# Two feed-forward products by Strassen's algorithm, with the sums of operands and products made beside them

## The chip, the cores and the metric

The kernel runs on one core of a Trainium2 chip. The time is the device time of one execution in microseconds (us), median of three runs. Everything is float32; the matrix products take each operand as a high and a low part (type fp32r) and add three products per pair.

## What is computed

Cut to what matters here: a cross-attention layer, and behind it a feed-forward layer on z, the normalized sum x + attention.

```python
x = x + xattn(layernorm(x), ctx)                      # x: (4, 512, 1024)
z = layernorm(x)
routing = sum(top_k(z @ gate_w, 2))                   # gate_w: (1024, 8)
h = relu(z @ up_w) ** 2                               # up_w: (1024, 2048)
shared = h @ down_w                                   # down_w: (2048, 1024)
routed = ((z @ fc1_w) @ expert_w * routing) @ fc2_w   # fc1_w: (1024, 512), expert_w: (512, 512), fc2_w: (512, 1024)
out = x + layernorm(shared + routed) * gamma + beta
```

## The kernel before, in words

The program has stages, one behind the other, with five engines that wait for each other by semaphores. Each stage has a function for each engine (`c_pe`, `c_dve`, and so on). `past(s, v)` is a semaphore and the count to wait for.

- **p0, a, b**: weights, layer norm, q, k and v, attention. The change leaves them as they are, but for two names that it takes from them.
- **c**, the output projection: 16 tiles of 128 rows (4 batches of 4). TensorE makes 12 k-steps x 2 halves x 3 parts = 72 matmuls a tile. The attention output comes from DRAM in four units a tile (`c_load_unit` on SyncE's queue). ScalarE makes a unit's high part (`c_units_hi`), GpSimd its low part (`c_units_lo`). A unit's place is free again when TensorE has used it in the tile before. VectorE adds x to the finished tile (`c_dve`, L1607), SyncE stores it. Batch 1 also folds `expert_w` and `fc2_w` into one matrix `w_d`. Beside the last two batches VectorE normalizes z of batches 0 and 1 (`d_norm`), ScalarE stores it and reads it back in blocks (`d_z_out` L1342, `d_blocks_in` L1350), and VectorE turns the blocks (`d_turn` L1362).
- **d**, the up products: for each batch 16 chunks of `up_w` and 4 of `fc1_w`, each with 8 k-steps x 3 parts = 24 matmuls of 128x512 (`mm_groups`, `D_GROUPS`). The weights are split once into a hi and a lo half in 16 slots and stay there for all batches; only the four fc1 chunks are loaded again. ScalarE applies relu, VectorE squares, ScalarE stores (`d_act`, `d_dve`). A gate product of 16 matmuls a batch is made behind the first group (L1701, L1702), behind a wait for the gate's weights (`d_gw`).
- **e**, the down products: 16 tiles of 128 rows, each 20 k-steps x 2 halves x 3 parts = 120 matmuls (`e_pe`, `step`). The weights stay on chip for all tiles. ScalarE scales the routed part by the routing weight, VectorE adds, takes the layer norm and adds x (`e_dve`, `tile`). The last tile has its second half cut into two pieces of 256 columns (`LAST`), and a chain made for it in `last_tile`.

`parts3` is where nearly all matmuls stand, L118 to L120:

```python
e.matmul(o, lh, rh, start=first, stop=False)
e.matmul(o, lh, rl, start=False, stop=False)
return e.matmul(o, ll, rh, start=False, stop=last)
```

## Time and profile before

| what | value |
|---|---|
| median of 3 runs | 2096.02 us (2095.66 to 2096.24) |
| span of the profiled execution, first to last instruction | 2094.0 us |
| own time of the profiled execution | not given; the span is 2.0 us under the median |
| TensorE busy | 2075.4 us (99% of the span), 9580 matmuls |
| VectorE, ScalarE, GpSimd busy | 803.9, 695.1, 754.5 us |
| DMA | 286.31 MB, mean 137 GB/s |

The profile has one line for each engine. A matmul's duration there is about 0.39 us for 512 columns, while the next one starts 0.23 us later: matmuls overlap in the array, so what one costs is read from the distance of the starts. The feed-forward stages take the last 43% of the span, from about 1200 us on. A group's line in the rows below gives its count, its busy time, the mean of one instruction, and the idle time ahead of it with what ended it.

### The profile page before, as it was taken

How to read it: one execution, taken by the hardware profiler on the slowest of the kernel's cores; microseconds unless marked ns; L12 is line 12 of the kernel's file. 1: busy time of each engine (PE TensorE's matmuls, PEld its weight loads, DVE VectorE, ACT ScalarE, POOL GpSimd, SP SyncE). 2: the span in 40 equal slices, each digit the busy share in tenths (PEclk: the TensorE clock that was granted, in tenths of full speed). 3: DMA queues.
4: the chain of work that ended last, by engine and by line, in shares of the span. 5: the costliest groups of instructions: out<-in, count | busy, mean ns of one | idle time of the engine just before them, and what ended most of it. 6: DMA issues, size and time to landing. Idle time of an engine off the chain costs nothing.

```text
span 2094.0 us, 30294 instructions
## 1 busy us (share of the span) xinstructions
PE 2075.4 (99%) x9580; PEld 1732.2 (83%) x9580; DVE 803.9 (38%) x1419; ACT 695.1 (33%) x1209; POOL 754.5 (36%) x616
## 2 busy tenths in 40 slices
PE   8999999999999999999999999999999999999998
PEld 7888888888888888878888878787878888888887
DVE  4221312178888888831121412313231232222222
ACT  5121111167777777741111223112123311111111
POOL 2533030147777777662222343010024322222221
PEclk9999999999999999999999999999999999999999
DMA  6843433635655655544347555253434622222222
GB/s 198 265 158 140 154 117 111 179 83 147 159 151 150 160 154 137 130 121 146 131 156 198 200 157 156 105 150 111 133 97 134 211 87 89 90 88 83 76 82 76
DMA packets 302751, 286.31 MB, mean 137 GB/s; under 512 B 146896, under 2 KB 214480, under 8 KB 301776
## 3 DMA queue, kind: packets, MB, share of 16 engines
q1 hardware_dynamic: 188128, 196.58, 30.2%
q10 hardware_dynamic: 114544, 88.76, 15.3%
q8 instruction: 40, 0.66, 0.1%
q14 instruction: 39, 0.32, 0.1%
HBM read 184.32 MB, written 100.68 MB: 136 GB/s over the span
## 4 chain that ended last, share of the span: by engine, by line
PE 94%; DMA 2%; DVE 1%; POOL 1%; ACT 1%; issue 0%; ACTq 0%; SPq 0%; DVEq 0%; POOLq 0%
PE psum L118 29%; PE psum L119 29%; PE psum L120 29%; PE psum L988 3%; DMA staging<-in_up_w 1%; POOL operands L1281 1%; PE psum L1035 1%; PE psum L1015 1%; PE psum L1034 1%; PE psum L1016 1%; DMA staging<-in_fc_w 1%; DMA staging<-in_ctx 0%; ACT operands L1276 0%; PE psum L1702 0%; PE psum L1701 0%
## 5 line engine op out<-in xcount | busy, mean ns | idle before, releaser
L118 PE MATMUL psum<-operands 128*128 128x512 f32 (+3 forms) x2904 | 1115.7, 384 | 11.4 <-DVE operands L353 10.0
L119 PE MATMUL psum<-operands 128*128 128x512 f32 (+3 forms) x2904 | 1113.6, 383 | 0.0
L120 PE MATMUL psum<-operands 128*128 128x512 f32 (+3 forms) x2904 | 1111.0, 383 | 0.0
L118 PEld LDWEIGHTS psum<-operands 128*128 128x128 f32 (+1 forms) x2904 | 546.5, 188 | 111.5 <-DVE operands L353 9.8
L120 PEld LDWEIGHTS psum<-operands 128*128 128x128 f32 (+1 forms) x2904 | 546.9, 188 | 105.4
L119 PEld LDWEIGHTS psum<-operands 128*128 128x128 f32 (+1 forms) x2904 | 547.5, 189 | 94.0
L1281 POOL TENSOR_TENSOR operands<-staging,operands 128x512 fp32r<-128x512 f32 x92 | 118.6, 1301 | 349.3 <-ACT operands L1276 348.3
L1162 DVE TENSOR_REDUCE small<-psum 128x1 fp32r<-128x576 f32 x256 | 192.9, 754 | 89.8 <-PE psum L988 89.7
L1940 POOL TENSOR_TENSOR operands<-operands 128x640 fp32r<-128x640 f32 x64 | 100.6, 1574 | 319.1 <-ACT operands L1935 318.9
L905 POOL TENSOR_TENSOR operands<-staging,operands 128x512 fp32r<-128x512 f32 x128 | 164.6, 1293 | 30.4 <-ACT operands L1082 21.6
L1791 DVE TENSOR_TENSOR staging<-staging 128x512 f32<-128x512 f32 x64 | 46.6, 747 | 327.6 <-ACT staging L1749 326.8
L1935 ACT ACTIVATE operands<-operands 128x640 fp32r<-128x640 f32 x64 | 47.3, 740 | 284.4 <-DMA operands<-h_scratch 284.4
L1496 POOL TENSOR_TENSOR operands<-operands 128x384 fp32r<-128x384 f32 x64 | 65.7, 1032 | 183.7 <-ACT operands L1491 183.3
L1075 ACT ACTIVATE staging<-psum 128x512 f32<-128x512 f32 (+1 forms) x192 | 110.4, 589 | 27.2 <-DVE psum L1190 23.6
L1276 ACT ACTIVATE operands<-staging 128x512 fp32r<-128x512 f32 x92 | 56.4, 631 | 178.5 <-DMA staging<-in_up_w 59.2
L988 PEld LDWEIGHTS psum<-operands 96*128 96x128 f32 x512 | 95.5, 189 | 23.0 <-DVE small L1162 1.7
L1082 ACT ACTIVATE operands<-staging 128x512 fp32r<-128x512 f32 (+1 forms) x192 | 112.8, 620 | 0.0
L988 PE MATMUL psum<-operands 96*128 96x288 f32 x512 | 110.2, 297 | 0.1
L907 POOL TENSOR_TENSOR operands<-staging,operands 64x512 fp32r<-64x512 f32 x64 | 82.5, 1289 | 62.7 <-ACT operands L1082 59.2
L637 DVE SCALAR_TENSOR_TENSOR staging<-psum,staging 128x512 fp32r<-128x512 f32 (+1 forms) x40 | 26.5, 662 | 189.1 <-ACT staging L632 189.1
L1071 ACT ACTIVATE psum<-psum 128x512 f32<-128x512 f32 x128 | 74.6, 583 | 62.9 <-PE psum L120 59.6
L1491 ACT ACTIVATE operands<-operands 128x384 fp32r<-128x384 f32 x64 | 33.1, 524 | 177.8 <-DMA operands<-o_scratch 170.5
(123 smaller groups left out, 1285.0 us busy)
## 6 DMA issues: line engine op xcount, KB each, us to landing
h_scratch<-staging ACTq DMA_DIRECT2D x80, 256.0 KB, 2.2
operands<-h_scratch SPq DMA_DIRECT2D x64, 320.0 KB, 3.1
operands<-recip_scratch SPq DMA_DIRECT2D x64, 192.0 KB, 4.0
o_scratch<-staging SPq DMA_DIRECT2D x64, 192.0 KB, 4.9
operands<-o_scratch SPq DMA_DIRECT2D x64, 192.0 KB, 2.9
operands<-q_hi_scratch ACTq DMA_DIRECT2D x14, 768.0 KB, 5.9
operands<-q_lo_scratch ACTq DMA_DIRECT2D x14, 768.0 KB, 6.0
staging<-in_x SPq DMA_DIRECT2D x20, 512.0 KB, 4.0
```

The costliest lines, as they stand in the source:

```text
L118: e.matmul(o, lh, rh, start=first, stop=False)
L119: e.matmul(o, lh, rl, start=False, stop=False)
L120: return e.matmul(o, ll, rh, start=False, stop=last)
L905: e.tensor_tensor(pt[j][1], pst[j // 2], raw(pt[j][0]), ALU.subtract).then_inc(b_lop, 1)
L907: e.tensor_tensor(pt[j][0][C:P], pst[j // 2][0:C], raw(pt[j][0][0:C]), ALU.subtract).then_inc(b_lop, 1)
L988: m = e.matmul(bank[:, h * TH:(h + 1) * TH], qp[p][0][0:HD, a * S + u * P:a * S + (u + 1) * P], kp[p][0][0:HD, h * TH:(h + 1) * TH], start ...
L1071: e.activation(bank, bank, ACT.Exp).then_inc(b_ex, 1)
L1075: e.activation(pst[j // 2][0:n], bank[0:n], ACT.Exp).then_inc(b_ex, 1)
L1082: e.activation(pt[j][0][0:n], pst[j // 2][0:n], ACT.Copy).then_inc(b_hia, 1)
L1162: e.tensor_reduce(nm[o % 2][:, u:u + 1], bank[:, 0:T], AX.X, ALU.max, negate=True).then_inc(b_mx, 1)
L1281: e.tensor_tensor(job_part(j, h, slot_lo), halves[h], raw(job_part(j, h, slot_hi)), ALU.subtract).then_inc(j_lo, 1)
L1940: e.tensor_tensor(eu[u][1], raw(eu[u][1]), raw(eu[u][0]), ALU.subtract).then_inc(e_lo, 1)
```

## The change

It computes both feed-forward products by Strassen's algorithm (in Winograd's form of the sums), one level deep: the matrices are cut in four blocks, and seven block products take the place of eight.

- **Up products (new d).** The rows are two batches against two batches, the inner dimension is cut in two, and the columns are pairs of chunks. There are 10 iterations: 5 column blocks (4 of `up_w`, 1 of `fc1_w`) for each of two pairs of batches (`q` = 0 for batches 0 and 1, `q` = 1 for batches 2 and 3). Each has seven products in the order 1, 5, 6, 2, 7, 3, 4. Each product is 2 x 4 x 3 = 24 matmuls of 128x512. Operands: z operands (128 x 2048 each) are made once for each `q`, by VectorE's sums `z_sum`, ScalarE's high part `z_hi` and low parts by VectorE (`z_lo`, products 1, 5, 6, 7, 3) or GpSimd (`z_lo_pool`, products 2, 4). Weight operands (128 x 1024 each) are made anew in every iteration: four sums (`w_sum_op`) and three low parts (`w_lo_op`) on VectorE, seven high parts on ScalarE, four low parts (`w_lo_pool`) on GpSimd. The products' sums (seven additions from PSUM or SBUF), the four squares, and, on GpSimd, five sums of h that serve as operands of the next product (`add`) come on top. All seven operands of h are stored.
- **Down products (new e).** Seven passes (2, 4, 1, 3, 6, 5, 7), each with 8 groups (pairs of row tiles) of 10 k-steps x 3 parts = 30 matmuls of 128x512. Weights are loaded, added and split anew for each pass. Results are gathered in 16 tiles in SBUF. The layer norm of a tile is made in pass 6 or 7; the last tile is normalized whole.
- **z.** z is normalized by five jobs (`z_norm`), turned on chip, and stored turned (`z_turned_out`, `z_part_out`); it is read back as operands. Batches 0 and 1 and the norm of batch 2 lie in stage c; the rest lies in iterations 0 to 3 of stage d.
- **Gate.** 16 matmuls for batches 0 and 2, 24 for batches 1 and 3 (80 in place of 64). The wait for the gate's weights (`d_gw`) now stands ahead of stage d's first product.

The core of the diff, new code only (the old bodies of stages d and e are taken out; line numbers of the rest shift by 20 to 40):

```diff
+        ORDER = [1, 5, 6, 2, 7, 3, 4]
+        Z_SUMS, Z_HI, Z_LO_V, Z_LO_G = [5, 6, 7, 4], [1, 6, 5, 7, 2, 3, 4], [1, 5, 6, 7, 3], [2, 4]
+        W_SUMS, W_HI, W_LO_V, W_LO_G = [5, 6, 7, 3], [1, 5, 6, 2, 7, 3, 4], [5, 1, 6], [7, 2, 3, 4]
...
+        def d_first_loads(e):
+            e.wait_ge(*past(z_tw, 16))
+            z_load_op(e, 0, 1)
+            e.wait_ge(*past(z_tw, 32))
+            e.wait_ge(*past(f_lo, NQ))
+            z_stage(e, 0, "b12")
+            w_stage(e, 0)
+            z_stage(e, 0, "b22")
...
         def c_sp_eng(e):
...
+                    if n == LAST_C - 2:
+                        d_first_loads(e)
...
         def c_act(e):
...
+                if n in (7, 11):
+                    z_blocks_in(e, 2 * ((n - 7) // 4))
+                if n:
+                    c_units_hi(e, n, (2, 3))
+                if n in (7, 11):
+                    z_blocks_in(e, 2 * ((n - 7) // 4) + 1)
...
+                if n in (9, 13):
+                    z_turned_out(e, (n - 9) // 4)
+            z_hi(e, 0, 1)
...
         def c_dve(e):
...
+            z_sum(e, 0, 5)
+            w_sum_op(e, 0, 5)
+            z_sum(e, 0, 6)
+            z_lo(e, 0, 1)
+            tile(LAST_C - 1)
+            z_sum(e, 0, 7)
+            w_sum_op(e, 0, 6)
+            w_sum_op(e, 0, 7)
+            w_lo_op(e, 0, 5)
+            w_lo_op(e, 0, 1)
+            z_lo(e, 0, 5)
+            tile(LAST_C)
+            z_sum(e, 0, 4)
+            w_sum_op(e, 0, 3)
+            z_lo(e, 0, 6)
+            w_lo_op(e, 0, 6)
+            z_lo(e, 0, 7)
+            z_lo(e, 0, 3)
...
+        def d_pe(e):
+            e.wait_ge(*past(d_gw, 19))
+            for it in range(NIT):
+                q, dc = it // NF5, it % NF5
+                for s, p in enumerate(ORDER):
+                    if dc == 0:
+                        z_done(e, q, p)
+                    w_done(e, it, p)
+                    n, b = NP * it + s, 2 * q + dc - 1
+                    slot_free(e, n - 4)
+                    if dc in (1, 2) and p == 5:
+                        e.wait_ge(*past(d_gl, b + 1))
...
+                    product(it, s, 0)
+                    product(it, s, 1)
...
+        def d_dve(e):
...
+            for it in range(NIT):
...
+                if it:
+                    h21(it - 1)
+                if dc in (1, 2):
+                    gate_out(2 * q + dc - 1)
+                if it == NF5:
+                    z_sum(e, 1, 4)
+                    z_lo(e, 1, 6)
...
+                if nxt:
+                    w_sum_op(e, it + 1, 5)
+                if it == NF5 - 1:
+                    z_sum(e, 1, 5)
+                u_sums(it)
+                if nxt:
+                    w_sum_op(e, it + 1, 6)
+                    w_lo_op(e, it + 1, 5)
...
+                u5_sums(it)
+                if it == NF5:
+                    z_lo(e, 1, 7)
+                    z_lo(e, 1, 3)
+                if it == NF5 - 1:
+                    z_sum(e, 1, 6)
+                    z_lo(e, 1, 1)
+                if it in (0, 3):
+                    for i in range(4):
+                        z_turn(e, 5 if it == 0 else 7, i)
+                h11(it)
+                h22(it)
+                if nxt:
+                    w_sum_op(e, it + 1, 7)
+                    w_lo_op(e, it + 1, 1)
+                if it == NF5 - 1:
+                    z_sum(e, 1, 7)
+                h12(it)
+                if nxt:
+                    w_sum_op(e, it + 1, 3)
+                    w_lo_op(e, it + 1, 6)
+                if it == NF5 - 1:
+                    z_lo(e, 1, 5)
...
+        def d_pool(e):
...
+                e.wait_ge(*h_ready(it, "22"))
...
+                add(it, 1, OM1, O11, O22, ALU.add)
+                if nxt:
+                    w_lo_pool(e, it + 1, 7)
+                e.wait_ge(*h_ready(it, "12"))
...
+                add(it, 2, OM2, O12, O22, ALU.add)
+                add(it, 3, O12, O12, O11, ALU.subtract)
+                if nxt:
+                    w_lo_pool(e, it + 1, 2)
+                if it == NF5 - 1:
+                    z_lo_pool(e, 1, 2)
+                e.wait_ge(*h_ready(it, "21"))
...
+                add(it, 4, OM5, O11, O21, ALU.add)
+                add(it, 5, O21, O21, O22, ALU.subtract)
+                if nxt:
+                    w_lo_pool(e, it + 1, 3)
+                    w_lo_pool(e, it + 1, 4)
+                if it == NF5 - 1:
+                    z_lo_pool(e, 1, 4)
...
+        PASSES = [2, 4, 1, 3, 6, 5, 7]
+        NPR = B * ST // 2
...
+        def e_pool(e):
+            for g in range(NPR * NPASS):
...
+                    e_unit_lo(e, 2 * g + NU)
+                if PASSES[s] in (6, 7):
...
+                    e.tensor_tensor(x1b[i % NX], x1b[i % NX], bet, ALU.add).then_inc(e_xb, 1)
...
+                    e_unit_lo(e, 2 * g + NU + 1)
```

Two places in the order of the instructions. **VectorE at the seam of stages c and d, before**: the end of the norm of batch 1, the last addition of x (L1607), and the gate's weights (L1822 to L1826).

```order
581 L209 TENSOR_SCALAR staging<-staging,small 128x1024 [waits d_chain]
582 L209 TENSOR_SCALAR staging<-staging,small 128x1024 x3
583 L1607 TENSOR_TENSOR staging<-psum,staging 128x1024 [waits c_x_loaded,c_unit_used]
584 L1822 CAST operands<-small 128x8x8 [waits d_gate_weights]
585 L1824 TENSOR_TENSOR operands<-small,operands 128x8x8 [waits d_gate_weights]
586 L1826 MEMSET small 128x128 [waits d_gate_weights]
587 L1791 TENSOR_TENSOR staging<-staging 128x512 [waits d_staged,d_gate_weights]
```

The same place now (L1574 is the last addition of x; L1768 and L1829 are the sums for z operand 4 and weight operand 3, L1784 and L1841 low parts of z and of weights, L2153 to L2157 the gate's weights):

```order
598 L1784 TENSOR_TENSOR operands<-plain_2048,operands 128x2048 [waits z_operands_hi]
599 L1574 TENSOR_TENSOR staging<-psum,staging 128x1024 [waits c_x_loaded,c_unit_used]
600 L1768 TENSOR_TENSOR plain_2048<-plain_2048 128x2048 [waits z_sums,a_x_tile1,c_unit_used]
601 L1829 TENSOR_TENSOR plain_1024<-plain_1024 128x1024 [waits w_sums,a_stored1,c_unit_used]
602 L1784 TENSOR_TENSOR operands<-plain_2048,operands 128x2048 [waits z_sums,z_operands_hi]
603 L1841 TENSOR_TENSOR operands<-plain_1024,operands 128x1024 [waits w_operands_hi]
604 L1784 TENSOR_TENSOR operands<-plain_2048,operands 128x2048 [waits z_operands_hi] x2
605 L2153 CAST operands<-small 128x8x8 [waits d_gate_weights]
606 L2155 TENSOR_TENSOR operands<-small,operands 128x8x8 [waits d_gate_weights]
607 L2157 MEMSET small 128x128 [waits d_gate_weights]
```

Between the last addition and the gate's weights there are now six more instructions, and the first product of stage d waits for all of them: on TensorE it has this row.

```order
3109 L141 MATMUL psum<-operands 128x512
3110 L139 MATMUL psum<-operands 128x512 [waits w_operands_lo_by_dve,fold_staged,z_operands_lo_by_dve,d_gate_weights]
3111 L140 MATMUL psum<-operands 128x512
3112 L141 MATMUL psum<-operands 128x512
3113 L139 MATMUL psum<-operands 128x512
```

Before, TensorE began stage d without that wait (L118 waits for the first weight slot), and the gate's weights were waited for 72 matmuls later, at L1701.

```order
3112 L1685 ISA [waits d_zlo]
3113 L118 MATMUL psum<-operands 128x512 [waits d_up_slots,d_staged]
3114 L119 MATMUL psum<-operands 128x512
3115 L120 MATMUL psum<-operands 128x512
3116 L1685 REGISTER_ALU
```

**VectorE at the change to the second pair of batches**, end of iteration 4 and beginning of iteration 5 (L1784 are low parts of z: operand 5, then 6, then 7 and 3; L1768 is the sum for z operand 4; L2109 and L2103 are h21, L2121 is u_sums, L1819, L1823 weight sums):

```order
755 L1784 TENSOR_TENSOR operands<-plain_2048,operands 128x2048 [waits z_operands_hi]
756 L2109 TENSOR_TENSOR staging<-psum,staging 128x1024 [waits d_products]
757 L2103 TENSOR_TENSOR staging<-staging,plain_1024 128x512 [waits d_gate_spread,d_sums]
758 L2103 TENSOR_TENSOR staging<-staging,plain_1024 128x512
759 L1768 TENSOR_TENSOR plain_2048<-plain_2048 128x2048 [waits z_sums,a_x_tile1,d_products]
760 L1784 TENSOR_TENSOR operands<-plain_2048,operands 128x2048 [waits z_sums,z_operands_hi]
761 L1819 TENSOR_TENSOR plain_1024<-staging,plain_1024 128x1024 [waits w_a21_a22_staged,d_products]
762 L2121 TENSOR_TENSOR staging<-psum,staging 128x1024 [waits b_o_stored1,d_h_sums,d_p1_out,d_products]
763 L1823 TENSOR_TENSOR plain_1024<-plain_1024 128x1024 [waits w_sums,a_stored0,d_products]
764 L1841 TENSOR_TENSOR operands<-plain_1024,operands 128x1024 [waits w_operands_hi]
765 L2126 TENSOR_TENSOR staging<-staging 128x1024 [waits d_p5_out,d_sums]
766 L1784 TENSOR_TENSOR operands<-plain_2048,operands 128x2048 [waits z_operands_hi] x2
```

The operands of products 5, 6, 7 and 3 of iteration 5 are made in this order, after product 4 of iteration 4 has begun. The kernel before has nothing here to set beside it: its z of the next batch was split beside the last group of a batch, and no weight was split.

## Rows read from the trace of the kernel before

**Rows 1.** The page, busy time of the engines.
```profile
PE 2075.4 (99%) x9580; PEld 1732.2 (83%) x9580; DVE 803.9 (38%) x1419; ACT 695.1 (33%) x1209; POOL 754.5 (36%) x616
```

**Rows 2.** Waits of PE: us in total, times, longest (the two largest).
```profile
PE psum L118 <- DVE operands L353: 10.0, 7, 6.2
PE psum L118 <- POOL operands L1496: 0.9, 1, 0.9
```

**Rows 3.** Timeline of PE (start us, us, engine line op), two matmuls in stage c.
```profile
1195.21 0.39 PE L120 MATMUL psum<-operands 128*128 128x512 f32 x1
...
1207.45 0.39 PE L120 MATMUL psum<-operands 128*128 128x512 f32 x1
```

**Rows 4.** Timeline at the end, last tile: PE, and ACT's queue with the last stores.
```profile
2085.98 0.28 PE L120 MATMUL psum<-operands 128*128 128x256 f32 x1
...
2086.70 0.28 PE L120 MATMUL psum<-operands 128*128 128x256 f32 x1
...
2090.84 1.00 ACTq L2066 DMA_DIRECT2D out<-staging  x2
```

**Rows 5.** Groups by line and form: busy us, mean ns | idle before.
```profile
L1607 DVE TENSOR_TENSOR staging<-psum,staging 128x1024 f32<-128x1024 f32 x16 | 19.6, 1225 | 163.0 <-PE psum L120 163.0
L2104 DVE SCALAR_TENSOR_TENSOR staging<-staging,small 128x1024 f32<-128x1024 f32 x15 | 19.3, 1284 | 2.4 <-DVE small L2103 0.4
L1427 DVE TENSOR_TENSOR operands<-staging,operands 128x1024 fp32r<-128x1024 f32 x4 | 4.9, 1226 | 36.4 <-ACT operands L1414 36.4
L1423 DVE TENSOR_TENSOR operands<-staging,operands 128x2048 fp32r<-128x2048 f32 x1 | 2.3, 2283 | 0.0
L1414 ACT ACTIVATE operands<-staging 128x1024 fp32r<-128x1024 f32 x4 | 4.2, 1062 | 26.7 <-DMA staging<-in_fc_w 26.7
L1940 POOL TENSOR_TENSOR operands<-operands 128x640 fp32r<-128x640 f32 x64 | 100.6, 1574 | 319.1 <-ACT operands L1935 318.9
L1281 POOL TENSOR_TENSOR operands<-staging,operands 128x512 fp32r<-128x512 f32 x92 | 118.6, 1301 | 349.3 <-ACT operands L1276 348.3
```

**Rows 6.** Timeline of DVE, ACT and its queue: seam of c and d, and earlier.
```profile
1114.71 4.12 ACTq L1350 DMA_DIRECT2D staging<-z_scratch  x8
...
1150.76 1.23 DVE L1607 TENSOR_TENSOR staging<-psum,staging 128x1024 f32<-128x1024 f32 x1 [15.10 <-PE psum L120]
...
1153.27 0.53 ACT L1491 ACTIVATE operands<-operands 128x384 fp32r<-128x384 f32 x1 [3.65 <-DMA operands<-o_scratch]
...
1200.86 0.18 DVE L1822 CAST operands<-small 128x64 fp32r<-128x64 f32 x1
```

**Rows 7.** DMA issues: KB each, median us to landing.
```profile
z_scratch<-staging ACTq DMA_DIRECT2D x4, 2048.0 KB, 7.8
staging<-in_x SPq DMA_DIRECT2D x3, 2048.0 KB, 7.7
operands<-o_scratch SPq DMA_DIRECT2D x64, 192.0 KB, 2.9
```

**Rows 8.** Timeline of DVE and POOL where both read SBUF.
```profile
1661.62 1.30 DVE L1887 TENSOR_TENSOR operands<-staging,operands 128x512 fp32r<-128x512 f32 x2
1662.32 2.02 POOL L1940 TENSOR_TENSOR operands<-operands 128x640 fp32r<-128x640 f32 x1 [2.00 <-ACT operands L1935]
1663.06 1.83 DVE L1887 TENSOR_TENSOR operands<-staging,operands 128x512 fp32r<-128x512 f32 x1
```

**Rows 9.** Timeline of PE at the kernel's first matmuls.
```profile
6.21 0.58 PE L118 MATMUL psum<-operands 128*128 128x256 f32 x1 [6.21 <-DVE operands L353]
...
6.81 0.41 PE L120 MATMUL psum<-operands 128*128 128x256 f32 x1
...
10.01 0.41 PE L120 MATMUL psum<-operands 128*128 128x256 f32 x1
```

More of the change, by code:

```diff
@@ L71, in mmf, with plain @@
             return MM[p0:p0 + p, a:a + n]
+        def plain(a, n):
+            first, size = min((at for at in PLAIN if at[0] <= a and a + n <= sum(at)), key=lambda at: at[1])
+            return pieces[first, size][:, a - first:a - first + n]
         def raw(ap):
@@ L108, in sem, with later @@
             return s
+        Later = namedtuple("Later", ("sem", "base"))
+        def later(s, last):
+            return Later(s, last)
         def past(s, v):
-            return s, v + credits[s.name][1]
+            s, base = s if isinstance(s, Later) else (s, 0)
+            return s, base + v + credits[s.name][1]
         idle = es.enter_context(nc.semaphore("idle"))
@@ L1571, in c_bank0 @@
+            z_hi(e, 0, 1)
+        def c_pool(e):
+            for n in range(1, B * ST):
+                c_units_lo(e, n, range(4) if n > 1 else (2, 3))
         def c_bank0(n):
-            return 4 if n == B * ST - 1 else 2 * (n % 2)
+            return 2 * (n % 2)
         def c_step(e, n, t, k):
@@ new lines, in xattn_ffn_kernel, with pair @@
+        STORED_AS = {0: 3, 1: 4, 2: 6, 3: 7, 4: 1, 5: 2, 6: 5}
+        def pair(bank):
+            return PS[:, bank:bank + 2, :].rearrange("p b n -> p (b n)")
+        a_uses_of = [16 * sum(ring(n) == r for n in range(NF + 2 * QC)) for r in range(NR)]
+        heads = NH // (2 * G)
+        za_ld = {p: later(a_ld_t[i], 16) for i, p in enumerate((1, 2, 3))}
+        zb_ld = {n: later(b_row[i], 64 * NH // 2) for i, n in enumerate(("b12", "b22"))}
+        zs_s, zh_s = sem("z_sums"), sem("z_operands_hi")
@@ L1647, in xattn_ffn_kernel @@
+        d_hs = sem("d_h_sums", 5)
+        d_os = [later(b_os[i], 16 * heads) for i in range(7)]
+        d_gw, d_gm, d_gl, d_gt = (sem(f"d_gate_{n}") for n in ("weights", "product", "staged", "turned"))
+        d_gc, d_rst, d_rld = sem("d_gate_chain"), sem("d_gate_stored"), sem("d_gate_spread")
+        GW = mmf(45056, DK * 2 * NE).rearrange("p (k e) -> p k e", k=DK)
         gTs = sm[:, 216:216 + P]
@@ new lines, in slot_bank, with slot_free @@
+        def slot_bank(n):
+            return 2 * ((n + 2) % 4)
+        def slot_free(e, n):
+            if n < 0:
+                if n >= -2:
+                    e.wait_ge(*past(cc_x1, B * ST + n + 1))
+                else:
+                    e.wait_ge(*past(f_ev, NQ))
+                return
+            it, p = n // NP, ORDER[n % NP]
+            if p == 1:
+                e.wait_ge(*past(d_s1, it + 1))
+            elif p == 5:
+                e.wait_ge(*past(d_s5, it + 1))
+            else:
+                e.wait_ge(*summed(it, {6: "u", 2: "c11", 7: "c22", 3: "c12", 4: "c21"}[p]))
@@ new lines, in xattn_ffn_kernel, with w_half, w_plain, sums_v @@
+        e_gb, e_xb, e_st = sem("e_gamma_beta"), sem("e_x1_beta"), sem("e_stored")
+        e_xl = [later(s, 48 * heads) for s in b_vc] + [later(s, 16 * NH // 2) for s in b_s4 + b_rs[:1]]
+        SUMS_V = [0, 1, 2, 1, 1, 2, 1]
+        SUMS_A = [2, 1, 0, 1, 0, 0, 0]
+        E_CHAIN, E_ROOT = 9, 4
+        def w_half(s, j, hf):
+            return mmf(W_BASE[s % 2][j] + hf * D, D)
+        def w_plain(s, j):
+            return plain(W_BASE[s % 2][j] + D, D)
+        def sums_v(s, pr):
+            return NPR * sum(SUMS_V[:s]) + SUMS_V[s] * pr
@@ new lines, in e_x1_load, with e_first_loads @@
+        def e_x1_load(e, i):
+            e.wait_ge(*past(e_post, i - NX + 1))
+            row = ln_tile(i)[1] * P
+            e.dma_start(x1b[i % NX], x1_d[row:row + P, :]).then_inc(e_xl[i % NX].sem, 16)
+        def e_first_loads(e):
+            e.wait_ge(*after_product(NIT - 1, 1))
+            for j in range(3):
+                e_weights_load(e, 0, j)
+            e.wait_ge(*after_product(NIT - 1, 5))
+            for j in range(3, NPAIR):
+                e_weights_load(e, 0, j)
+            e_unit_load(e, 0)
+            e.wait_ge(*after_product(NIT - 1, 6))
+            for n in range(1, 4):
+                e_unit_load(e, n)
+            e.wait_ge(*after_product(NIT - 1, 2))
+            for n in range(4, NU):
+                e_unit_load(e, n)
@@ L2143, in e_dve @@
[L2143 to L2151 removed]
+                e.wait_ge(*past(e_xb, i + 1))
+                e.scalar_tensor_tensor(y, y, rstd[:, 0:1], x1b[i % NX], ALU.mult, ALU.add).then_inc(e_post, 1)
+                assert n[0] == E_CHAIN
```

1463 lines of the change are left out of this document (830 added, 633 removed).

## The prediction

> **What bounds the kernel now.** I read the page's busy times first: TensorE is busy for 2075.4 of 2094.0 us, no other engine for more than 39% [rows 1]. Then who waited for whom: TensorE's two largest sums of waits are 10.0 us, in the first stage, and 0.9 [rows 2]. So it is bound by TensorE's instructions, and what counts is the number of matmuls and the distance of their starts. Two starts 54 matmuls apart lie 12.24 us apart [rows 3], 0.2267 us each; the 0.39 us in the row is the time in flight. At 256 columns 6 starts take 0.72 us, 0.120 each [rows 4].
>
> **What the change takes from TensorE.** Before, the two stages have 1920 + 64 (gate) matmuls of 512 columns for the up products; for the down products 15 x 120 + 72 of 512 and 96 of 256. That is 3856 x 0.2267 + 96 x 0.120 = 885.7 us. Now it is 1680 + 80 + 1680 = 3440, 779.8 us. **Term 1: -105.9 us.** Nothing else is as sure.
>
> It pays only if TensorE still never waits. All sums, splits and additions must stay beside the matmuls, and they have grown. I therefore went through each engine's queue with the durations of rows 5.
>
> **One iteration of the up products** is 168 matmuls, 38.1 us. VectorE has 7 additions that read PSUM or SBUF (one of them both from SBUF), 4 squares, 4 weight sums, 3 low parts, each 128x1024 and 1.23 to 1.28 us [rows 5]: 18 instructions, 22.5 us. GpSimd has 9 of 128x1024. Its rows give 1.30 us for 512 columns and 1.57 for 640 [rows 5], so 0.27 for each further 128 and 2.39 us for 1024: 21.5 us. ScalarE has 9 at 1.06 [rows 5], 10 us. Each alone fits. But VectorE and GpSimd do not run freely beside each other. Where both work at once [rows 8], two subtractions of VectorE end at 1662.92; GpSimd's, begun at 1662.32, ends at 1664.34, 2.02 us instead of 1.57; VectorE's next, begun at 1663.06, takes 1.83 instead of 0.65 and ends 0.55 after GpSimd's. Each held the other for nearly its whole length, with about 0.15 saved at a change. VectorE's additions that read PSUM always took 1.225 [rows 5] and were not held.
>
> The Trainium skill ("SBUF — State Buffer", Who interferes with whom) says the same and more widely: a VectorE instruction with two SBUF inputs and a GpSimd instruction that reads SBUF exclude each other for the whole instruction. The trace agrees (1.83 for 0.65 us), and it is the rule that speaks most against this change.
>
> So 12 of VectorE's 18 (15.0 us) and all of GpSimd's (21.5) share 38.1 us; with 0.15 off at some 16 changes that is 34. Walked in the written order, from the end of one h22 to the next, I get 38.3, because GpSimd cannot begin before h22, and VectorE's u_sums waits for its fifth sum. It just keeps pace with TensorE, but nothing that comes late is made good. Every extra piece then costs. These are terms 3 and 4.
>
> **Term 2, stage c: +8.5.** ScalarE now issues 32 block loads in one tile. 8 took 4.12 us [rows 6], so 32 take 16.5, with four high parts of 0.53 18.6 against a tile's 16.3 (72 x 0.2267): the next unit comes about 1.5 late. And `d_first_loads` puts 3 MB into SyncE's queue ahead of tile 14's units, behind a wait for the 2 MB store of turned z. That store is issued behind the high part that comes 2.5 us after tile 12's addition [rows 6] and lands 7.8 later [rows 7], at about 11. By 2048 KB in 7.7 us and 192 KB in 2.9 [rows 7] the queue moves 387 KB a us: 3 MB are 7.9, the unit 2.9, its split 1.5: 23.4, against 16.3. TensorE waits 7. Bounds 0 (if the small load overtakes) and 12.
>
> **Term 3, start of the up products: +24.** The first product now waits for the gate's weights, which stand behind everything else on VectorE. When TensorE ends tile 15, VectorE still has 1.5 us of a low part of z, the addition 1.2, z sum 4 (2.2), weight sum 3 (1.2), low parts of z 6, 7, 3 (2.28 each [rows 5]), of w 6 (1.2), and 0.7 for the gate's three; before, that was the addition and the three, from 1200.86 on [rows 6], and TensorE went on. That is 15 to 16 us; four GpSimd low parts of 2.39 fall among them and hold it for 8 more. Lower bound 15, upper 28.
>
> **Term 4, the up products: +41.** Iteration 1: gate results are copied behind h21, at about 53 us of my walk, TensorE asks at 49: 4. Iteration 3: the four turns with DRAM round trips delay h22, so the weights of iteration 4 come 6 late. **The second pair of batches** (iterations 4, 5): VectorE's 20 us of z sums and low parts and GpSimd's 10 are made when the old operands fall free. Product 1 waits 4. Low part 5 ends 20 us after h22 (7 instructions of VectorE, 11.5, with four of GpSimd), when product 5 could have begun at 10: 10. Low part 6 comes 10 later against 5.4: 4. Low part 7 comes 22 later (seven of GpSimd, 16 us, and 6 of VectorE's), against two products, 10.9: 11. Sum 29, and 2 for the small lags behind. With no exclusion the same walk gives 14 in all.
>
> **Term 5, half clock: +9.** The kernel's first matmuls, behind 6.21 us of idleness, start 0.213 us apart (15 in 3.20 [rows 9]), 256 columns at 1.2 GHz, against 0.120 later [rows 4]. 18 of them cost 18 x 0.093 = 1.7 us. Five of the waits above last over 4 us (7, 24, 6, 10, 11): 5 x 1.8. Bounds 0 and 12.
>
> **Term 6, down products: +2 in the passes, +9 at the end.** A group is 30 matmuls, 6.8 us. GpSimd needs 3.15 (two units at 1.57) and in passes 6 and 7 a further 2.39; VectorE's norm there has two instructions of 1.28 with two SBUF inputs [rows 5], some 6.3 us with all, 8.4 with GpSimd's holds. It falls 1.6 behind in each of 8 groups; seven PSUM banks of slack hide that in pass 6, but not behind the last group: about 6. The whole last tile adds 3: from the last matmul to the end it was 7.0 us [rows 4], with half tiles; now 6.3 of chain and about 4 of store.
>
> DMA grows (all seven h operands stored, weights read again for each pass), to some 150 GB/s in the up products, well under the 387 KB a us above; I give it nothing.
>
> Sum: -105.9 + 8.5 + 24 + 41 + 9 + 11 = -12.4. The profiled span of 2094.0 becomes 2081.6; the median of the runs stands 2.0 above the span: **2084 us**.
>
> **The rivals.**
> - **The holds matter little** (25%). VectorE and GpSimd would wait only where they start together. For it: most rows of VectorE's multiplications in stage e stand at 1284 ns on average [rows 5], not stretched. Against it stand the holds of 1.14 and 0.45 us [rows 8]. Then term 3 is 16, term 4 is 14, term 6 is 3, term 5 is 5: 2084 - 8 - 27 - 8 - 4 = 2037.
> - **The pair VectorE and GpSimd becomes the bound of every iteration** (15%, slower). The 38.3 of my walk stands on 0.15 saved at each of 16 changes and on no cost for semaphores. Without the saving and with 0.05 for each hop the iteration takes 41.5, 3.2 over, in 8 iterations that have no other wait: 2084 + 26 = 2110. It is slower than before by more than 0.2% once an iteration takes about 40.2.
> - **The likeliest** (60%): as summed, with the bounds of the terms 2062 to 2104.
>
> That the products are not fewer is excluded: the order of instructions has 7 x 24 per iteration and 30 per group.
>
> **How the numbers follow.** 0.2% is 4.2 us, what a measurement here can tell: under 2091.8 is faster, over 2100.2 slower. Of the likeliest case (2062 to 2104, centre 2084) three quarters and a bit lie under 2091.8, 0.47; with the first rival 0.72. Same 0.10 (0.09 of the likeliest, 0.01 of the slower rival). Slower 0.18. The range reaches from the first rival, 2035, to 2106; 1 in 10 on either side is left out.
>
> **What would show it.** In the profile after: 3440 feed-forward matmuls 0.2267 apart where nothing waits; a gap of about 24 us ahead of the first up product, released by the gate's memset; gaps ahead of products 5 and 7 of iteration 5, released by VectorE's low parts; GpSimd and VectorE instructions of 1024 columns at up to 3.5 us where they meet; a last store about 16 us behind the last matmul. If the first gap is 15 us and GpSimd's mean stays at 2.4, the first rival holds. If TensorE waits in iterations 6 to 9 too, the second does. If TensorE's waits come to under 30 us in all, the walk is wrong.

## The result, and the profile after

The changed kernel takes **2123.6 us** (median of 4 runs, 2119.9 to 2126.1), the kernel before on the same chip 2095.8 (4 runs): ratio 1.0131, 95% interval 1.0116 to 1.0145. It is 1.3% slower; the forecast was 2084, with a range up to 2106. The profiled execution has a span of 2124.4 us, 30.4 more than the 2094.0 of before.

The page, busy times and the granted clock in 40 slices of 53.1 us:

```profile
PE 1998.0 (94%) x9068; PEld 1656.9 (78%) x9068; DVE 1251.8 (59%) x1611; ACT 747.1 (35%) x1194; POOL 1083.4 (51%) x686
...
PEclk9999999999999999999999889988899989999998
```

Against [rows 1], 512 matmuls fewer. But TensorE is no longer busy all the time, VectorE gained 448 us of busy time and GpSimd 329. Waits of PE from 958.7 us on, early in stage c (us in total, times, longest):

```profile
PE psum L139 <- POOL operands L2370: 24.4, 6, 12.6
PE psum L139 <- DVE operands L1784: 21.0, 2, 13.4
PE psum L139 <- DVE small L2157: 18.2, 1, 18.2
PE psum L139 <- POOL operands L1510: 13.3, 2, 10.8
PE psum L139 <- DVE operands L1841: 10.2, 1, 10.2
PE psum L139 <- issue: 4.6, 1, 4.6
PE psum L2000 <- DVE small L2074: 4.0, 2, 3.5
PE psum L139 <- ACT staging L2042: 1.9, 1, 1.9
```

That is 97.6 us where [rows 2] had 0.9 behind the first stage. L1510 is stage c's low parts, L2157 the memset behind the gate's weights, L1784 and L1841 low parts of z and of weights, L2074 the gate's copies, L2370 the low parts of the down products' units. By stretch (its length, busy us and count of PE, PEld, DVE, ACT and POOL, then the granted clock, the DMA share and GB/s): stage c from 958.7 us on, iterations 0 to 3 with the wait ahead of them, 4 and 5, 6 to 9, pass 1, passes 2 to 4, passes 5 and 6 of the seven (products 6 and 5), and the end:

```profile
958.70:1216.00 257.30, 243.97 (x1152) 204.98 (x1151) 77.30 (x110) 47.74 (x71) 53.42 (x51) 0.97 0.68 215
1216.00:1414.40 198.40, 166.49 (x716) 132.59 (x715) 161.83 (x145) 44.03 (x43) 112.37 (x37) 0.92 0.62 193
1414.40:1531.10 116.70, 90.93 (x353) 71.39 (x354) 102.86 (x52) 31.58 (x26) 77.15 (x24) 0.84 0.46 162
1531.10:1692.20 161.10, 158.74 (x700) 128.38 (x699) 124.32 (x93) 39.83 (x41) 106.96 (x38) 1.00 0.46 165
1692.20:1762.20 70.00, 57.44 (x242) 47.03 (x241) 32.02 (x17) 21.91 (x34) 42.92 (x22) 0.90 0.63 206
1762.20:1925.40 163.20, 163.20 (x722) 135.13 (x721) 76.48 (x68) 57.18 (x81) 81.78 (x48) 1.00 0.67 210
1925.40:2052.60 127.20, 115.24 (x482) 93.04 (x481) 105.26 (x124) 34.14 (x52) 81.81 (x40) 0.96 0.67 211
2107.10:2124.40 17.30, 0.04 (x1) 0.00 (x0) 13.34 (x30) 0.61 (x3) 0.54 (x1) 0.58 0.30 122
```

Where nothing is waited for, the products cost what was expected: passes 2 to 4 are 720 matmuls in 163.2 us, 0.2267 each. The loss lies at a few places, and the granted clock falls only in stretches with waits. A place from PE's timeline, behind the second wait of stage c:

```profile
1182.19 0.77 PE L139 MATMUL psum<-operands 128*128 128x512 f32 x1 [10.76 <-POOL operands L1510]
1182.75 0.63 PE L140 MATMUL psum<-operands 128*128 128x512 f32 x1
1183.18 0.63 PE L141 MATMUL psum<-operands 128*128 128x512 f32 x1
...
1185.19 0.39 PE L140 MATMUL psum<-operands 128*128 128x512 f32 x1
1185.41 0.39 PE L141 MATMUL psum<-operands 128*128 128x512 f32 x1
```

The starts are 0.43 us apart (1.2 GHz), a little later 0.22 to 0.23 (2.4 GHz). I counted 122 such matmuls from stage c on: 25.3 us over their price at full clock.

VectorE's and GpSimd's costly groups by form from 1216 us on (count | busy us, mean ns | idle before), and both engines' timeline in product 6's pass:

```profile
L1841 DVE TENSOR_TENSOR operands<-plain,operands 128x1024 fp32r<-128x1024 f32 x28 | 80.9, 2889 | 1.3 <-ACT operands L1837 1.3
L2096 DVE SCALAR_TENSOR_TENSOR staging<-staging 128x1024 f32<-128x1024 f32 x32 | 51.7, 1617 | 1.1
...
L2370 POOL TENSOR_TENSOR operands<-operands 128x640 fp32r<-128x640 f32 x112 | 201.9, 1812 | 173.1 <-ACT operands L2366 172.8
L2223 POOL TENSOR_TENSOR staging<-staging 128x1024 f32<-128x1024 f32 x50 | 149.2, 2986 | 145.8 <-DVE staging L2096 98.5 <-DVE staging L2103 45.7
L1847 POOL TENSOR_TENSOR operands<-plain,operands 128x1024 fp32r<-128x1024 f32 x40 | 129.9, 3258 | 31.8 <-ACT operands L1837 31.8
```

```profile
1976.84 4.04 POOL L2370 TENSOR_TENSOR operands<-operands 128x640 fp32r<-128x640 f32 x2
1978.00 1.38 DVE L2525 SCALAR_TENSOR_TENSOR small<-small 128x1 f32<-128x1 f32 x1
...
1979.60 1.30 DVE L2527 TENSOR_TENSOR small<-small 128x1 f32<-128x1 f32 x1
1979.72 0.72 ACT L2366 ACTIVATE operands<-operands 128x640 fp32r<-128x640 f32 x1
1980.85 2.36 POOL L2593 TENSOR_TENSOR staging<-staging 128x1024 f32<-128x1024 f32 x1
1980.94 3.36 DVE L2529 SCALAR_TENSOR_TENSOR plain<-plain,small,staging 128x1024 f32<-128x1024 f32 x1
```

A low part of 128x1024 that takes VectorE 1.23 us alone [rows 5] takes 2.89 on average. Even instructions on 128 numbers (L2525, L2527: 0.22 and 0.16 us elsewhere in the trace) last 1.3 to 1.4 beside a GpSimd instruction. ScalarE is not held: its high part of 128x1024 takes 1.055 us on average from 1216 us on, 1.062 before [rows 5].

### The profile page after: what moved, and what is told of

The parts are those of the page before. It is cut to its first block, busy times and chain, and to the rows that moved or that the text cites. A ratio compares the mean times of both kernels' runs of the same rounds, so it can differ in the third digit from the quotient of the medians.

```text
span 2124.4 us, 28447 instructions
## 1 busy us (share of the span) xinstructions
PE 1998.0 (94%) x9068; PEld 1656.9 (78%) x9068; DVE 1251.8 (59%) x1611; ACT 747.1 (35%) x1194; POOL 1083.4 (51%) x686
## 4 chain that ended last, share of the span: by engine, by line
PE 74%; DVE 10%; DMA 5%; issue 4%; POOL 3%; SPq 2%; ACT 1%; ACTq 1%; DVEq 0%; POOLq 0%
PE psum L139 22%; PE psum L140 22%; PE psum L141 22%; PE psum L1009 3%; POOL staging L2223 2%; DVE operands L1841 2%; DMA operands<-h_operand_scratch 2%; SPq L1355 1%; DMA operands<-o_scratch 1%; DMA z_turned_scratch<-plain 1%; ACTq L1355 1%; DVE plain L2523 1%; PE psum L1056 1%; PE psum L1036 1%; PE psum L1055 1%
## 5 line engine op out<-in xcount | busy, mean ns | idle before, releaser
L139 PE MATMUL psum<-operands 128*128 128x512 f32 (+3 forms) x2728 | 1062.2, 389 | 105.0 <-POOL operands L2370 24.4
L140 PE MATMUL psum<-operands 128*128 128x512 f32 (+3 forms) x2728 | 1058.3, 388 | 0.0
L141 PE MATMUL psum<-operands 128*128 128x512 f32 (+3 forms) x2728 | 1054.6, 387 | 0.0
L139 PEld LDWEIGHTS psum<-operands 128*128 128x128 f32 (+1 forms) x2728 | 519.3, 190 | 206.9 <-issue 34.9
L141 PEld LDWEIGHTS psum<-operands 128*128 128x128 f32 (+1 forms) x2728 | 519.6, 190 | 102.3
L140 PEld LDWEIGHTS psum<-operands 128*128 128x128 f32 (+1 forms) x2728 | 520.0, 191 | 89.9
L2370 POOL TENSOR_TENSOR operands<-operands 128x640 fp32r<-128x640 f32 x112 | 201.9, 1812 | 173.1 <-ACT operands L2366 172.8
L2223 POOL TENSOR_TENSOR staging<-staging 128x1024 f32<-128x1024 f32 x50 | 149.2, 2986 | 145.8 <-DVE staging L2096 98.5
L926 POOL TENSOR_TENSOR operands<-staging,operands 128x512 fp32r<-128x512 f32 x128 | 164.5, 1293 | 30.3 <-ACT operands L1103 21.5
L1510 POOL TENSOR_TENSOR operands<-operands 128x384 fp32r<-128x384 f32 x64 | 66.4, 1053 | 209.8 <-ACT operands L1505 209.8
L2366 ACT ACTIVATE operands<-operands 128x640 fp32r<-128x640 f32 x112 | 82.1, 737 | 237.3 <-DMA operands<-h_operand_scratch 237.2
L1847 POOL TENSOR_TENSOR operands<-plain,operands 128x1024 fp32r<-128x1024 f32 x40 | 129.9, 3258 | 31.8 <-ACT operands L1837 31.8
L1837 ACT ACTIVATE operands<-plain 128x1024 fp32r<-128x1024 f32 x70 | 72.3, 1054 | 200.9 <-DMA plain<-in_up_w 69.0
L540 POOL TENSOR_TENSOR staging<-staging 128x512 f32<-128x512 f32 x24 | 30.9, 1291 | 141.3 <-DMA staging<-moments_scratch 141.3
```

The source lines that it names most:

```text
L926: e.tensor_tensor(pt[j][1], pst[j // 2], raw(pt[j][0]), ALU.subtract).then_inc(b_lop, 1)
L1847: e.tensor_tensor(wL[p], wF[p], raw(wH[p]), ALU.subtract).then_inc(wlo_g, 1)
L2223: e.tensor_tensor(to, a, b, op).then_inc(d_hs, 1)
L2370: e.tensor_tensor(eu[n % NU][1], raw(eu[n % NU][1]), raw(eu[n % NU][0]), ALU.subtract).then_inc(e_lo, 1)
```

## The experiments

All are edits of the changed kernel (2123.6 us). Each was timed beside the kernel before, whose medians in the four sets were 2095.8 to 2096.5; ratios are to it.

**The gate's wait.**

```diff
-            e.wait_ge(*past(d_gw, 19))
             for it in range(NIT):
...
                     slot_free(e, NP * (it + 1) - 3)
+                    if it == 0:
+                        e.wait_ge(*past(d_gw, 19))
                     gate(2 * q + dc, it)
```

> Edit: TensorE waits for the gate's weights only ahead of the gate product of iteration 0, not ahead of the first up product. Theory A (the wait stands on the order of instructions alone): the gap of 18.2 us ahead of the first product goes, TensorE starts about 1216.5. Product 2 then comes at about 1232.7, and its low parts on GpSimd end at 1238.9 in the trace of the change: a new wait of about 6. Net -12, and no change of the half clock's cost: 2112 us. Theory B (VectorE and GpSimd are short of time, so a wait taken away here comes back at the next products): at most 4 us are won, 2120 us or more.

Measured: 2115.5 us, ratio 1.0096 (1.0079 to 1.0113). The gap of 18.2 us is gone, 6.4 came ahead of product 2 as worked out, and the gate's wait in iteration 1 grew from 3.5 to 6.4. Of 18 us 8 are won, between the two theories and nearer to the first: the order made the wait, but more than half of it returns at the waits behind.

**The queue ahead of the first down units.** Why pass 1 waits stands in the changed kernel's timeline, GpSimd first, then SyncE's queue:

```profile
1685.76 11.33 POOL L2370 TENSOR_TENSOR operands<-operands 128x640 fp32r<-128x640 f32 x5
1697.05 14.60 POOL L2223 TENSOR_TENSOR staging<-staging 128x1024 f32<-128x1024 f32 x5
1723.70 3.04 POOL L2370 TENSOR_TENSOR operands<-operands 128x640 fp32r<-128x640 f32 x2 [12.06 <-ACT operands L2366]
```

```profile
1689.43 22.57 SPq L1872 DMA_DIRECT2D h_operand_scratch<-staging  x7
...
1714.49 1.73 SPq L2362 DMA_DIRECT2D operands<-h_operand_scratch  x2
```

GpSimd makes six low parts, then the last five sums of h; SyncE's queue waits to store each sum (until 1712), and only then loads weights and unit 6, which TensorE wants at 1712. The edit moves four unit loads up:

```diff
+            for n in (NU, NU + 1):
+                e_unit_load(e, n)
             h_out_late(NIT - 1)
+            for n in (NU + 2, NU + 3):
+                e_unit_load(e, n)
             e.wait_ge(*past(d_hs, 5 * NIT - 1))
```

> Edit: SyncE's queue loads units 6 to 9 of the first down pass ahead of the last stores of h, for which GpSimd's last sums are waited for. Theory A (the queue's order makes the wait of 12.6 us in pass 1): the wait goes, with 13 matmuls at half clock behind it (2.8 us): 2108 us. Theory B (GpSimd is too late with the low parts because VectorE holds it): at least 8 us of the wait stay, 2118 us or more.

Measured: 2116.5, ratio 1.0101 (1.0084 to 1.0117). The wait of 12.6 fell to 0.5, and 4.5 came two groups later, where the next units stand behind the weights. Theory A, with half of the gain expected.

**The loads of x1 in SyncE's queue.** Each waits for a finished norm; the edit issues them two groups later (in product 6's pass for `pr - 3 + NX` in place of `pr - 1 + NX`, and so on).

> Edit: the loads of x1 that wait for a finished norm stand two groups later in SyncE's queue, so that unit loads no longer stand behind that wait. Theory A (queue order): the four waits in passes 5 and 6 (11.7 us) and 17 or more matmuls at half clock (5.5 us with those behind) go; the end behind the last matmul stays at 17: 2107 us. Theory B (VectorE and GpSimd hold each other there, low parts are late by themselves): the waits stay within 3 us: 2120 us or more. Between: the waits in the passes go but the norms are further behind at the end, so that the end grows from 17 by up to the 12 us won.

Measured: 2126.0, ratio 1.014 (1.0123 to 1.0157): no gain. The waits of passes 5 and 6 of the seven fell only from 11.8 to 9.3 us, and the end behind the last matmul grew from 17.2 to 22.1. Where the loads of x1 stood did matter: in the changed kernel SyncE's queue waits 51.5 us for finished norms in these two passes, in this run 11.1. But the norm holds the units back at a second place, in ScalarE's queue, which the edit left as it was. There a norm's square root (L2476) stands ahead of the next units' high parts (L2366) and waits for VectorE, in this run:

```profile
1980.21 0.20 ACT L2476 ACTIVATE small<-small 128x1 f32<-128x1 f32 x1 [8.46 <-DVE small L2521]
...
1980.32 0.72 ACT L2366 ACTIVATE operands<-operands 128x640 fp32r<-128x640 f32 x1
```

GpSimd stood idle for 5.1 us for that high part, and TensorE for 3.3 us for the low part behind it. No run moved the square root.

**Tile 14's units ahead of the 3 MB.** `c_load_unit` for the first two units of tile 14 moves into `d_first_loads`, ahead of `e.wait_ge(*past(z_tw, 32))`.

> Edit: the first two units of tile 14 are loaded ahead of the wait for the turned z and of the 3 MB behind it. Theory A (those 3 MB ahead of the unit in one queue make the wait of 10.8 us): the wait falls to 2 us or less, 9 to 10 us and 1 of half clock won: 2113 us. Theory B (the DMA engines are full whatever the order): the wait falls by less than 4: 2120 us or more. If VectorE's sums were what counted, the start of the up products moves later by what is won here.

Measured: 2125.0, ratio 1.0139 (1.0118 to 1.016). The wait at tile 14 fell from 10.8 to 2.3 and 2.5, so the 3 MB ahead of the units made most of it; but the wait for the gate's weights grew from 18.2 to 21.6, and nothing was won in all. With the wait at the start in place, the end of VectorE's queue set the start, which came 1.1 us earlier.

**GpSimd's five sums left out.** `e.tensor_tensor(to, a, b, op)` in `add` becomes `e.memset(to, 0.0)`, so five of seven operands of h are not computed.

> Edit: GpSimd's five sums of h (128x1024, two SBUF inputs) become memsets of the same tiles, so that the output differs; all else stays. Theory A (VectorE and GpSimd hold each other for whole instructions, and this makes the waits of iterations 3 to 5): VectorE's mean for squares falls from 1617 ns towards 1230, and the waits behind the start of the up products (3.5 + 10.2 + 4.6 + 7.6 + 1.5 + 13.4 + 0.5 + 1.9 = 43 us) fall to 15 or less: with half clock 2088 us. Theory B (those waits are made by the order of instructions and by DRAM round trips, holds only shift them): they stay above 30: 2110 us or more.

Measured: **2079.3**, ratio 0.9928 (0.9911 to 0.9945), 44 us less. In this run:

```profile
L1841 DVE TENSOR_TENSOR operands<-plain,operands 128x1024 fp32r<-128x1024 f32 x29 | 37.4, 1288 | 2.3 <-ACT operands L1837 2.3
L2096 DVE SCALAR_TENSOR_TENSOR staging<-staging 128x1024 f32<-128x1024 f32 x32 | 54.8, 1711 | 1.1
```

VectorE's low parts of weights, untouched by the edit, fell from 2889 to 1288 ns; the squares stayed held (1711; I had expected 1230), now by other GpSimd instructions. The waits behind the start fell from 41.7 (the 43 above has 1.5 too much) to 17.7 (15 expected) and the 12.6 of pass 1 fell to 0.2, since GpSimd is free there. GpSimd lost work (a memset of 128x1024 takes 0.95 us, a sum took 2.99), and VectorE lost holds and no instruction. So this shows the pair's time as the cause; the run does not tell how much of it was GpSimd's own work and how much the holds.

**Order in iteration 5.** Why product 7 waits 13.4 us: VectorE idles 7.2 us for GpSimd's sum, which stands behind two low parts of z.

```profile
1482.22 7.84 POOL L1792 TENSOR_TENSOR operands<-plain,operands 128x1024 fp32r<-128x1024 f32 x2 [4.30 <-DVE plain L1768]
1490.03 4.87 POOL L2223 TENSOR_TENSOR staging<-staging 128x1024 f32<-128x1024 f32 x2
```

The edit puts `z_lo_pool(e, 1, 2)` behind `add(it, 5, ...)`, and `z_lo(e, 1, 7)` and `z_lo(e, 1, 3)` ahead of `u_sums`.

> Edit: GpSimd makes z's low part 2 behind the last two sums of iteration 4 (it stood ahead of them), and VectorE makes z's low parts 7 and 3 ahead of the first sum of iteration 5, in which it now idles 7.2 us for GpSimd's sum. Theory A (order): the wait of 13.4 us ahead of product 7 falls to 5 or less, with up to 4 new ahead of product 2: 2119 us. Theory B (the pair is full there, only less work helps): the sum of waits of iteration 5 stays within 3 us of 27: 2122 to 2125 us.

Measured: 2119.5, ratio 1.0109 (1.0092 to 1.0125), as Theory A had it; 4 us are little beside the spread of the runs (2116.8 to 2121.4), so the waits in the trace are the better evidence. The wait of 13.4 is gone, with 3.5 new ahead of product 6 and 1.4 ahead of product 2; the waits of iteration 5 fell from 25.6 to 18.3, and in iteration 6 a wait for the gate grew to 4.6.

**Transposes in the waits.** Ahead of 12 waits, 763 in all (the text below counts 824), for instance:

```diff
+            slot_free(e, -4)
+            for _ in range(150):
+                e.transpose(PS[:, slot_bank(0), 0:P], ident[:], ident[:])
             e.wait_ge(*past(d_gw, 19))
```

> Edit: no wait is changed, but TensorE is given 824 transposes of the identity (0.11 us each at full clock) into the bank of the coming product, ahead of 12 of its waits, so many as fill 80 to 95% of each. Theory A (idleness ahead of the matmuls costs the clock): the 124 matmuls at half clock (25 us over their price) fall to 30 or fewer: 2104 us. Theory B (the half clock has another cause, such as the power drawn over longer times): the number stays above 90: 2122 us or more. If the transposes themselves run at half clock (0.21 us) they would outlast the waits: slower than 2124.

Measured: 2115.0, ratio 1.0091 (1.0074 to 1.0108). In PE's timeline, and over iterations 4 and 5:

```profile
1214.51 16.54 PE L1986 MATMUL psum<-ident 128*128 128x128 f32 x150
1232.81 0.50 PE L139 MATMUL psum<-operands 128*128 128x512 f32 x1 [1.77 <-DVE small L2169]
```

```profile
1414.40:1531.10 116.70, 107.77 (x563) 89.64 (x563) 103.41 (x62) 30.55 (x25) 79.89 (x25) 0.97 0.46 163
```

The granted clock there rose from 0.84 to 0.97, matmuls at half clock fell from 122 to 26, and with them 20.9 us of TensorE's time. The theory on idleness holds; but the whole got only 8.6 us faster, where I had expected 20. Most waits end when VectorE or GpSimd is done, so matmuls that end sooner wait longer. With the transposes' time counted in (0.110 us each), the waits of iteration 5 grew from 25.6 to about 31 us, those of passes 5 and 6 of the seven from 11.8 to about 16.

**Squares on ScalarE.**

```diff
-                e.scalar_tensor_tensor(h, h, 0.0, h, ALU.max, ALU.mult).then_inc(d_f, 1)
+            e.activation(h, h, ACT.Relu).then_inc(d_rl, 1)
+            e.wait_ge(*past(d_rl, n_sq[0]))
+            e.activation(h, h, ACT.Square).then_inc(d_f, 1)
```

> Edit: the 32 squares of h (relu and square in one instruction of VectorE, 1617 ns on average in the trace of the change) are made by ScalarE in two instructions, relu and square; nothing else. ScalarE is 35% busy. Theory A (the pair VectorE and GpSimd is what the up products wait for): 52 us less of VectorE's work shorten the waits behind the start of the up products from 43 to 25 or less, GpSimd's mean of 3.0 us falls; with half clock 2098 us. Theory B (dependency chains and orders, not the pair's time): a square takes two ScalarE instructions of about 1.05 us and is 0.5 us or more later: no gain or a loss, 2120 to 2130 us.

Measured: 2107.3, ratio 1.006 (1.0044 to 1.0075), 16 us less (25 expected). The five sums of GpSimd, unchanged, now:

```profile
L2232 POOL TENSOR_TENSOR staging<-staging 128x1024 f32<-128x1024 f32 x50 | 134.1, 2683 | 161.4 <-ACT staging L2016 117.4 <-DVE staging L2120 42.5
```

2683 in place of 2986 ns. The result lies between the theories. The waits behind the start fell to 27.7: iteration 4's from 10.2 to 5.2, iteration 1's went, but product 6 of iteration 5 got 6.0, and product 7 kept 11.7.

**GpSimd's additions of beta earlier.** Five of them in pass 4 of the seven, which has room, three in product 6's pass, five in product 5's, three in the last; the x1 loads nearly as in the run on them alone (in product 5's pass they follow each other one group apart and not two).

> Edit: GpSimd adds beta to x1 for tiles 0 to 4 in pass 3, for 5 to 7 in pass 6, for 8 to 12 in pass 5 and for 13 to 15 in pass 7, in place of eight in pass 6 and eight in pass 7; loads of x1 as in the run in which they alone stood later. Theory A (in pass 6 GpSimd's low parts and VectorE's norms lock each other, and GpSimd's additions are what makes it too much): the waits of passes 6 and 5 fall from 12 (12.8 with the loads alone) to 4 or less, the end behind the last matmul from 17 (22) to 13: 2108 us. Theory B (the waits come from loads or weights in SyncE's queue): the waits stay above 9 and only the end is shorter: 2120 us.

Measured: 2109.4, ratio 1.0067 (1.0053 to 1.0081), 14.2 us less. PE's waits in the stretch of passes 5 and 6 of the seven:

```profile
PE psum L139 <- POOL operands L2370: 5.3, 6, 2.1
```

In the same view the changed kernel has 11.8 and the run with the loads alone 9.3 (the 12.8 above was misread), and the end fell from 17.2 (22.1 with the loads alone) to 12.6. The matmuls at half clock behind these waits (about 5 us by my count) nearly all went too. Set beside the run with the loads alone, this shows that the additions in these two passes made about half of the waits that were left and the longer end. The 5.3 left lie in product 5's pass.

**All orders together.** The gate, the first units, tile 14, iteration 5, the turns of iteration 3 behind h22 and h12, the additions of beta.

> Edit: those of the gate's wait, of the first down units, of tile 14's units and of iteration 5 together; the turns of the last z block stand behind h22 and h12 of iteration 3; and GpSimd adds beta to x1 for five tiles in pass 3 and for five in pass 5 instead of all in passes 6 and 7. Theory A (orders make the waits; each gain adds up): -8 (gate) -7 (units) -8 (tile 14, now that the start no longer waits for the gate) -8 (iteration 5) -5 (turns) -10 (passes 5, 6 and the end): 2078 us. Theory B (the pair VectorE and GpSimd is the bound from stage c's end to iteration 5, so that what is won ahead is waited for later): only the gains in the down products add up: 2100 us.

Measured: 2091.7 (10 runs, 2087.0 to 2097.4), ratio 0.9981 (0.9971 to 0.9991): between the theories, 0.2% under the kernel before. The single gains do not add up to the 46 expected; the gate product of iteration 0 now waits 8.9 us for h22, product 2 of iteration 4 waits 5.9, and waits in iteration 5 stay at 20.

**All orders and squares on ScalarE**, and in iteration 3 the last turned blocks' stores behind the weights' load.

> Edit: the squares on ScalarE together with all changes of order, and in SyncE's queue of iteration 3 the second pair of turned blocks behind the loads of weights. If both kinds of gain add up: 2091.7 less 15 to 25 us, 2070 us, faster than the kernel before. If the orders already gave what the pair's shortage cost: 2088 to 2092 us.

Measured: **2064.0** (5 runs, 2063.3 to 2065.8), ratio **0.9845** (0.9832 to 0.9859). It beats both kernels. The squares, with the one change of stores, are worth 27.7 us here, where they gave 16.3 alone. Its waits from stage c on, the largest:

```profile
PE psum L139 <- DVE operands L1784: 10.6, 2, 8.2
PE psum L139 <- issue: 9.9, 3, 7.4
PE psum L139 <- POOL operands L2395: 9.9, 7, 4.5
PE psum L1977 <- DVE staging L2162: 8.0, 1, 8.0
PE psum L139 <- POOL operands L1510: 7.8, 3, 3.1
```

47.9 us in all, and 71 matmuls at half clock.

**The same with transposes in six waits** (198 in all; the text below says seven).

> Edit: the best version so far with 198 transposes of the identity in seven of its waits. If the half clock behind the waits costs the end what it did in the run with transposes alone (8.6 us for 21 us of half clock taken away, 0.4 for each): 16.5 us of half clock fall to 5, 2064 - 5 = 2059 us. If it costs one for one: 2053 us. If the waits simply grow by what the matmuls save: 2063 us.

Measured: 2067.2 (4 runs, 2064.2 to 2072.8), ratio 0.9872: not faster than without; of the three numbers expected the last, 2063, is nearest. 51 matmuls remained at half clock, the last matmul of the profiled execution ended 0.7 us earlier. Only some 5 us of half clock were taken away, and the runs spread over 8.6 us, so this run gives no gain that could be told apart from none. It agrees with the run above: where another engine sets the pace, a clock kept up is worth little.

## Why the prediction was wrong

Its terms beside what TensorE's rows in the profiled execution show:

| step | predicted | measured |
|---|---|---|
| 1, fewer matmuls | -105.9 | -105.9 (0.2267 each in passes 2 to 4) |
| 2, stage c | +8.5 | +13.3 (2.57 and 10.76) |
| 3, start of the up products | +24 | +18.2 |
| 4, up products | +41 | +41.7 |
| 5, half clock | +9 | +25.3 (122 matmuls) |
| 6, waits in the down passes | +2 | +24.4 |
| 6, end | +9 | +10.2 (17.2 for 7.0) |
| a wait begins 0.16 late, at the end of the 0.39 in flight | none | +2.4 (15 waits) |
| sum | -12.4 | +29.6, of 30.4 in the span |

- **The step that failed most is term 6, waits in the down passes, 22 us too small.** I priced one group of the passes and the backlog behind the last one, and asked nothing of the seam between iteration 9 and pass 1. There SyncE's queue had waits for GpSimd's last sums ahead of the next units: 12.6 us, of which the run with the loads moved up won back 7. In the passes of products 6 and 5 I took 1.6 us of lag per group to be hidden by seven PSUM banks. The runs show 11.8 us of waits there, 2.65 in product 6's pass and 9.17 in product 5's, which I had given no term. What runs out is not banks but low parts of units: GpSimd's additions and the norm's instructions lock each other, and the late norm holds the units back in SyncE's and ScalarE's queues. With the additions spread and the loads later 5.3 are left. How the rest divides between the lock and ScalarE's queue was not tested.
- **Term 5 is mis-sized, 16 us too small.** The price of one wait was about right (1.8 said, 2.1 measured: 25.3 us on 12 waits that slow the clock); their number was not. I had counted waits of over 4 us and five of them. Here 12 waits had slow matmuls behind them, among them some of 2.1 and 2.6 us. What the half clock costs the end is another number: taking 20.9 us of it away gave 8.6.
- **Term 2**: the mechanism was right (moving the units took the 10.8 down to 2.3 and 2.5). The unit came 11 us after its issue at 1169.4, not at my 387 KB a us. The working has 18.6 us of ScalarE against a tile's 16.3, which is 2.3 late and not 1.5; measured 2.6. That the wait of 10.8 cost the end nothing while the start waited for the gate is what I had not seen: terms 2 and 3 are not independent.
- **Term 3**: right in kind and inside its bounds. GpSimd held VectorE there only at the gate's two small instructions (2.36 and 2.29 us); before them it was the other way round (below).
- **Term 4** is right in size and nearly so in place; that the sum agrees to 1 us is in part luck, since iteration 4 was 4 too low and iteration 5 3 too high. Predicted and measured: iteration 1, 4 and 3.5; iteration 4, 6 and 10.2; iteration 5, 29 and 25.6 (4.6, 7.6, 13.4); small lags, 2 and 2.4.
- **The end** was 9 predicted and 10.2 measured, but my working gives no reason why a lag of 1.6 us in each of 8 groups should leave 6. The additions and the loads of x1 moved took the end from 17.2 to 12.6 us, so a part of it was theirs.
- **The rivals.** I read a hold of 1.14 us off [rows 8]; 1.83 less 0.65 is 1.18, which changes nothing. That holds matter little fell: GpSimd's mean is 2986 and 3258 ns, not 2.4 us. That every iteration is bound by the pair fell as well: iterations 7 and 8 take 38.2 and 38.1 us with no wait, and iterations 6 and 9 have waits of 0.5 and 1.9. The pair is short only where z, norms or additions of beta come on top.
- **The direction.** The gain forecast, 12 us, is smaller than the error of term 6 alone. Terms 5 and 6 together are 38 us too small. The chance for faster, 0.72, treated the places I had walked as all there were.

## What to carry to other kernels

Where a change takes 5% off the bounding engine and adds half to the work of two others that lock each other, count every instruction of both in each stretch, and walk the seams between stages and every in-order queue there before the steady state. Several waits behind one slow engine are not additive: removing one moves part of it to the next, so test them together. Work that can go to an engine outside the lock (here squares to ScalarE) was worth more than keeping TensorE's clock up (16.3 us against 8.6).

## What the runs showed of the hardware that I had not expected

**GpSimd can wait through several VectorE instructions.** At the start of the up products:

```profile
1221.64 10.33 POOL L1847 TENSOR_TENSOR operands<-plain,operands 128x1024 fp32r<-128x1024 f32 x1 [17.22 <-ACT operands L1837]
...
1225.25 4.48 DVE L1784 TENSOR_TENSOR operands<-plain,operands 128x2048 fp32r<-128x2048 f32 x2
1229.66 2.36 DVE L2153 CAST operands<-small 128x64 fp32r<-128x64 f32 x1
```

A low part of about 2.4 us lasted 10.33 (10.60 at the same place in the run with the gate's wait moved) while four subtractions of VectorE followed each other without a hold. I had assumed a change of hands at each instruction. Then GpSimd got in, and a cast of 64 columns, 0.18 us before [rows 6], took 2.36. That one has a single SBUF input. The Trainium skill ("SBUF — State Buffer", Who interferes with whom) counts casts among the instructions that can enter a mode with two ports and then contend; this row agrees. Its sentence that whoever issues first gets the ports for the whole instruction fits the alternation at 1976 to 1984. Here GpSimd was passed over four times in a row.

**The clock's loss does not grow with the wait.** Waits of 2.6, 10.8 and 18.2 us had 8, 6 and 11 matmuls at half clock behind them. Nor is a short wait sure to cost anything: the same wait in stage c, of 2.7 to 3.1 us in seven other runs, had none behind it. The wait of 10.8 us, 11.3 in the run with the gate's wait moved, had about 12 there. Transposes of 128 columns of the identity, 0.110 us apart (150 in 16.54 us), kept the granted clock at full through an 18 us wait.
